# GNN, attention and mixture-of-experts layer on one Trainium2 core: which engine waits for the stores, and where the last weight transfer is cut

## The reference

```python
h = _masked_grouped_mm(routed_in.astype(jnp.bfloat16), w_up.astype(jnp.bfloat16), onehot)
h = jnp.square(jax.nn.relu(h.astype(jnp.bfloat16)))
routed_out = _masked_grouped_mm(h.astype(jnp.bfloat16), w_down.astype(jnp.bfloat16), onehot)
...
hs = jnp.square(jax.nn.relu(xf @ shared_w_up.T))
shared_out = hs @ shared_w_down.T
...
out = combined.reshape(-1, TOP_K, dim).sum(axis=1) + shared_out
```

## Time and profile before

| | |
|---|---|
| median of 3 runs | 360.12 us (360.01 to 360.24) |
| the profiled execution, its own time | 361.38 us |
| its span, first to last instruction | 359.6 us |
| outside the span | 1.78 us |
| TensorE matmul busy | 312.3 us (87%) |
| VectorE, ScalarE, GpSimd busy | 111.3, 59.0, 48.6 us |
| bytes moved by transfers | 104.90 MB |
| stores of the result | 192, 120, 48 and 24 KB |

### The profile page before, as it was taken

The page is one execution under the profiler, slowest core; times in us unless marked ns, Lnnn a source line. Parts: engine busy times, 40 slices in busy tenths (PEclk is TensorE's granted clock), DMA queues, the critical chain, the costliest instruction groups (busy, mean ns, idle before and its releaser), DMA issues.

```text
span 359.6 us, 3130 instructions
## 1 busy us (share of the span) xinstructions
PE 312.3 (87%) x1236; PEld 152.2 (42%) x1236; DVE 111.3 (31%) x246; ACT 59.0 (16%) x113; POOL 48.6 (14%) x90
## 2 busy tenths in 40 slices
PE   4999998999999999999689998899998883474666
PEld 4334444334343343433254455543455551242334
DVE  7608605501152539121822113210222240111111
ACT  1401000001003010300020023310223340121131
POOL 0512110212112211142300001110001120000000
PEclk9999999999999999999959999999999996876888
DMA  7999999999999999999999999999999999999995
GB/s 289 366 298 379 341 339 359 356 340 419 313 314 424 341 281 417 327 386 361 273 330 248 284 428 318 213 218 215 206 213 228 217 216 218 221 211 216 207 215 125
DMA packets 13288, 104.90 MB, mean 292 GB/s; under 512 B 1600, under 2 KB 2328, under 8 KB 4060
## 3 DMA queue, kind: packets, MB, share of 16 engines
q0 software_dynamic: 11808, 98.57, 95.6%
q1 hardware_dynamic: 1168, 6.01, 4.3%
q10 hardware_dynamic: 300, 0.16, 0.2%
HBM read 150.48 MB, written 0.39 MB: 420 GB/s over the span
## 4 chain that ended last, share of the span: by engine, by line
PE 79%; DMA 12%; DVE 3%; another core or an unknown queue 3%; ACT 2%; issue 1%
PE bank L828 43%; DMA stage<-in_expert_up 12%; PE bank L995 9%; PE bank L1012 8%; PE bank L970 6%; PE bank L1043 5%; PE bank L797 1%; PE bank L958 1%; PE bank L836 1%; PE bank L812 1%; PE bank L949 1%; ACT xn L437 1%; DVE xn L759 1%; PE bank L1024 0%
## 5 line engine op out<-in xcount | busy, mean ns | idle before, releaser
L828 PE MATMUL bank<-ring,xnt 128*96 128x512 f32 x224 | 100.5, 607 | 0.6 <-ACT xnt L373 0.6
L828 PEld LDWEIGHTS bank<-ring,xnt 128*96 128x96 f32 x224 | 36.8, 167 | 58.9 <-issue 57.9
L1012 PE MATMUL bank<-stage,hbuf 128*96 128x512 bf16 (+3 forms) x242 | 45.6, 349 | 17.1 <-DMA stage<-in_expert_down 14.0
L995 PE MATMUL bank<-stage,late 128*96 128x512 bf16 (+1 forms) x192 | 44.3, 384 | 10.1 <-DMA stage<-in_expert_up 9.6
L828 PE MATMUL bank<-ring,stage 128*96 128x512 f32 x96 | 42.1, 593 | 0.0
L1012 PEld LDWEIGHTS bank<-stage,hbuf 128*96 128x96 bf16 x242 | 26.6, 131 | 34.6 <-issue 18.4
L995 PEld LDWEIGHTS bank<-stage,late 128*96 128x96 bf16 x192 | 24.0, 130 | 26.8 <-issue 14.7
L772 DVE TENSOR_TENSOR acc<-acc_t,acc 96x512 f32<-96x512 bf16 (+3 forms) x22 | 11.9, 543 | 55.9 <-ACT acc_t L460 55.6
L437 ACT ACTIVATE xn<-bank 96x512 bf16<-96x512 f32 (+2 forms) x26 | 14.6, 560 | 76.6 <-PE bank L995 59.3
L828 PEld LDWEIGHTS bank<-ring,stage 128*96 128x96 f32 x96 | 15.3, 163 | 22.9 <-issue 22.9
L759 DVE TENSOR_TENSOR xn<-xn 96x512 bf16<-96x512 bf16 (+1 forms) x24 | 9.6, 399 | 44.3 <-ACT xn L437 44.3
(11 more groups left out here) (160 smaller groups left out, 207.4 us busy)
## 6 DMA issues: line engine op xcount, KB each, us to landing
stage<-in_expert_down POOLq DMA_DIRECT2D x7, 1408.0 KB, 23.1
stage<-in_expert_up POOLq DMA_DIRECT2D x3, 2816.0 KB, 29.5
stage<-in_expert_down POOLq DMA_DIRECT2D x3, 2816.0 KB, 36.0
stage<-in_expert_up POOLq DMA_DIRECT2D x6, 1024.0 KB, 12.3
ring<-in_shared_down POOLq DMA_DIRECT2D x2, 2816.0 KB, 11.6
ring<-in_shared_up POOLq DMA_DIRECT2D x5, 1024.0 KB, 13.9
ring<-in_mat_wq SPq DMA_DIRECT2D x4, 1024.0 KB, 9.5
ring<-in_mat_wv POOLq DMA_DIRECT2D x4, 1024.0 KB, 10.4
```

Of the source, the lines that this page charges most:

```text
L828: ins = mm(bank[BANKS[m] + h][0:N, :], tiles(src)[:, k, :], w[:, kk, :], start=(k == 0), stop=(k == KT - 1))
L995: ins = mm(bank[4 + j][0:N, 0:c1 - c0], tiles(xe)[:, k, :], w[:, k, :], start=(k == 0), stop=(k == KT - 1))
L1012: ins = mm(bank[j][0:N, 0:c1 - c0], tiles(e_h)[:, t, :], w[:, t, :], start=(t == 0), stop=(t == TT - 1))
```

## The change

Two things are changed. The wait for the four stores goes from SyncE's program to the end of GpSimd's. And the last cut of the fine down weights moves: the third transfer now holds block 2 (128 columns) and tiles 0 to 5 of block 3 (64 columns), the fourth only tiles 6 to 10 of block 3. Places in memory and the number of transfers stay as they are. `load` takes offsets in elements of a partition in place of columns. As the third transfer now writes into the place of block 3, the waits before the transfers are each one block later (`min(j + 2, 4)`). TensorE waits for the fourth transfer before tile 6 of block 3 rather than before tile 0.

```diff
+EARLY = 6
+FINE_CUTS = [0, 512 * TT, 832 * TT, 960 * TT + EARLY * 64, D * TT]
...
-    UP_LOADS + [(0, 8, 11, 1)] + [(1, c0, c1, 2 + j) for j, (c0, c1) in enumerate(FINE)] if e == 1 else
-    UP_LOADS + [(0, 8, 11, 0)] + [(1, c0, c1, 1) for c0, c1 in HALVES])]
+    UP_LOADS + [(0, 8, 11, 1)] + [(1, FINE_CUTS[j], FINE_CUTS[j + 1], 2 + j) for j in range(len(FINE))] if e == 1 else
+    UP_LOADS + [(0, 8, 11, 0)] + [(1, c0 * TT, c1 * TT, 1) for c0, c1 in HALVES])]
...
-            sp.wait_ge(out_landed, 16 * len(FINE))
...
-                f0, f1 = (x0 * UNIT, x1 * UNIT) if m == 0 else (x0 * TT, x1 * TT)
+                f0, f1 = (x0 * UNIT, x1 * UNIT) if m == 0 else (x0, x1)
...
-                    load(e, 1, 0, D, 1)
+                    load(e, 1, 0, D * TT, 1)
...
-                    for j, (c0, c1) in enumerate(FINE):
-                        pool.wait_ge(down_done, DOWN_BEFORE[e - 3] + j + 1)
-                        load(e, 1, c0, c1, 2 + j)
+                    for j in range(len(FINE)):
+                        pool.wait_ge(down_done, DOWN_BEFORE[e - 3] + min(j + 2, len(FINE)))
+                        load(e, 1, FINE_CUTS[j], FINE_CUTS[j + 1], 2 + j)
+            pool.wait_ge(out_landed, 16 * len(FINE))
...
-                    if blocks is FINE:
+                    if blocks is FINE and j < len(FINE) - 1:
                         pe.wait_ge(stage_landed[b][2 + j], turn * 16 + 16)
...
                     for t in range(TT):
+                        if blocks is FINE and j == len(FINE) - 1 and t == EARLY:
+                            pe.wait_ge(stage_landed[b][2 + j], turn * 16 + 16)
                         ins = mm(bank[j][0:N, 0:c1 - c0], tiles(e_h)[:, t, :], w[:, t, :],
                                  start=(t == 0), stop=(t == TT - 1))
```

## The result

The changed kernel takes 367.06 us in the median of 6 runs (366.48 to 368.33), the kernel before 360.11 in runs beside it. The ratio is 1.0187, 95% interval 1.0175 to 1.0200: slower by 6.95 us, and well outside the predicted range of 359.6 to 360.7. The profiled execution took 366.48 us, with a span of 364.7.

The account below looks back on a forecast made before the run. The last experts run at the pace of the transfers, and only the 3.7 us from last landing to end can shorten. +0.25 (cut) - 0.22 (wait on GpSimd) = +0.03 us on 360.12 gave 360.1 us, range 359.6 to 360.7.

Parts of the forecast that it names:

- the price of the wait on GpSimd: Closing meeting: last landing to the end of GpSimd's drain changes from 0.59 us; -0.22 us taken.
- low end: Closing meeting: GpSimd leaves the wait like SyncE and drains in 0.17 us; 0.37 in place of 0.59, -0.22 us.
- high end: Closing meeting: GpSimd wakes 0.30 us late, then 0.2, then 0.4 of drain; 0.90 us in all, +0.31.
- rival B: Closing meeting: GpSimd's drain keeps its length wherever it stands; slower, 360.37 to 360.68 us; chance 0.30.
- The cut: Expert 7's last blocks: the third transfer lands 0.47 us later and delays block 2; +0.25 us.
- rival D: Expert 7's last transfers: the last landing decides, the third slips less than its bytes say; -0.51, 359.61 us; chance 0.10.
- The later issues: GpSimd's issue of the four transfers one block later, hidden by the queue's depth; put at 0.
- C: Expert 7's last blocks: TensorE late by its clock, so the cut costs nothing; 359.90 us; chance 0.13.
- A: Whole kernel: the forecast itself, 360.1 us, cut and wait on GpSimd as two terms that cancel; chance 0.42.
- E: GpSimd's issues: the later ones reach a queue that has run short; up to +1.50, 361.6 us; chance 0.05.
- slower: Whole kernel: slower by over 0.2% (over 360.84 us), by a short queue or a drain beyond 1.06 us; chance 0.06.
- The waking: Closing meeting: GpSimd wakes from its wait 0.30 us late, as for an issue, possibly by software dispatch on eight cores.

Follow-up runs that it names:

- the probe: The kernel before with pairs of GpSimd drains added at five places, from its first software transfer to its last issue; 379.24 us in a single run.
- the early drain: The kernel before with the wait for the stores moved to GpSimd and a GpSimd drain added ahead of it, behind its last issue; 360.47 us, ratio 1.0011.
- the early wait: The kernel before, SyncE still waiting for the stores, with GpSimd waiting for expert 7's up matmuls before its closing drain; 360.13 us, ratio 0.9993.
- both waking tries: The kernel before with GpSimd's drain, wait for expert 7's first-block sum, memset, then stores wait; the second adds the cut with two early tiles; 360.55 and 360.35 us.

## Why the prediction was wrong

**The step that failed is the price of the wait on GpSimd.** It put the time from the last landing of a store to the end of GpSimd's drain at 0.37 us (low end) to 0.90 (high end); the profile after has 6.9, of which 6.75 are the drain. Both ends came from rows that are no bound. The opening drain of 0.17 us has no software transfer ahead of it; GpSimd's drains with nothing open ahead of them take 0.04 to 0.17 in these runs. The 0.4 us between SyncE's word and the end of the closing drain was read as something that SyncE's word sets off. It was the last piece of a second pass of 3.39 us that the last landing of the weights had set off at 355.93. I named the drain of 69 us in rival B as the one thing that the trace did not explain, and then priced it by its last 0.4 us. For an operation whose record is that long, the upper bound is the record, not its tail.

What I lost with it is what sets the end. In the kernel before, this is not the stores. The drain ends at 359.32, SyncE is ready at 358.9: the work behind the last landing had 0.4 us to spare. The wait on GpSimd puts the two in a row, stores (2.9 us behind the landing), then both passes of the drain. From the last landing to the end of the span there were 3.6 us before (355.93 to 359.55) and 10.1 after (354.62 to 364.7), 6.4 more; with the wait alone 10.5 (355.71 to 366.2), 6.9 more. The medians say 6.95 and 6.84. They need not agree to the tenth: the last landing itself moves from execution to execution, and one profile is one execution.

**The cut** went as worked out. The third transfer lands 0.42 us before the fourth (0.39 expected), TensorE stands 0.40 us before block 2 (the 0.35 and the 0.04 behind it in the chain above; about 0.4 expected), and 22 matmuls take 1.31 (1.33 expected). Block 3 is done 0.93 us behind the last landing in place of 0.74: +0.19, where the sum had +0.25. In the whole time no price can be measured (ratio 1.0001 for the cut alone), and the traces say why: in that run GpSimd's drain ended at 358.38 and SyncE's at 358.07, so the drain covers the 0.19. For the same reason the gain that I allowed for in rival D could not have come.

**The later issues** cost nothing that the same run can show, as predicted. They were not run apart from the cut, but in the profile after the four transfers still spend 61 to 66 us between issue and landing.

**The rivals.** None held the result. B had the right object, GpSimd's drain, and the right sign, at 360.37 to 360.68. It stopped at 0.90 us from landing to drain's end, where 6.9 were measured. C, TensorE late by its clock, does occur: with the wait alone the granted clock was 0.50 from 349.8 to 353.2, blocks 0 to 3 ran without a break, and block 3 was done 1.06 us behind the last landing in place of 0.74. In the profile after, the clock was 1.00 from 352.0 on and TensorE waited for the third transfer. C and D differ from A only in the price of the cut, and a few tenths there decide nothing beside 6.75. E was wrong. The chance of 0.06 for "slower" was far too low for a step whose nearest rows were of other situations.

**The waking.** The high end also held an extra step of GpSimd's waking. It does not show: the last store landed at 357.52 and GpSimd's branch stands at 357.55. The Trainium skill, "GPSIMD Engine Reference", section 2.1 Instruction dispatch, has each of GpSimd's eight cores look up an instruction's handler in software. Nothing of that is seen between a semaphore and a branch here.

## What to carry to other kernels

If GpSimd issues the loads, its drain at the end takes time: here 0.04 us per transfer, once from its start and once again when the last load has landed. So let GpSimd come to the end of its program early, and put waits for stores on an engine that has no such drain (SyncE here); and when looking for the last microseconds, compare the end of GpSimd's drain with the end of the stores before shortening either. A record that is open for tens of microseconds on an engine believed idle hides a cost of unknown size: bound it by its whole length, or by what it may be waiting for.

## What the runs showed of the hardware

- A drain of GpSimd does not end before its software transfers have landed: 12, 16, 16 and 70 us in the probe, with the ends 0.1, 0.6, 1.1 and 1.8 us behind the last landing. It waits for its broadcasts too: 3.71 us for three of them, with no transfer open.
- The time behind the landing grows with the transfers since the last drain: 0.09 us for 1, 0.58 for 13, 1.06 for 25, 1.55 for 37, 1.80 for 43, 3.06 for 74 and 3.39 for 82. One line, 0.045 + 0.0408 n, gives all seven to 0.01 us. The 3.39 came in six kernels with the drain begun early: the one before, the cut alone, the early drain, the early wait and both waking tries. It does not go by bytes: 37 transfers of 51.9 MB take 0.030 us per MB, 74 of 87.0 MB take 0.035, while both take 0.041 to 0.042 per transfer.
- Begun after or shortly before the last landing, it takes twice that: 6752 ns in the changed kernel, with the wait alone, with a second drain behind it, and when begun 0.6 us early; 3077 ns with 37 transfers. A second drain behind it takes 0.04 to 0.05 us.
- What a pass does, and whether it goes by transfers or by their rows, stays open: all of these transfers have 128 rows (the queue has 144 packets per transfer with 82, 74 and 37 of them), so the two were never told apart.
- An instruction of GpSimd behind such a drain waits for it, even if its semaphore is long there: the memset at 358.82 for a semaphore of about 355.2.
